# Feature-major queries and keys, and a new order of the work on every engine, in a two-layer attention kernel

## The reference, cut to what matters

```python
h = ln(x);  q, k, v = h@wq+bq, h@wk+bk, h@wv+bv     # 16 heads of 16; q scaled by 0.25
q, k = rope(q), rope(k)                              # rotates halves of each head by the row number
x = x + softmax(q k^T, causal) v @ wo + bo           # self attention
h = ln(x);  q from h;  k, v from y (the context)     # cross attention, rope on q and k, no mask
x = x + softmax(q k^T) v @ wo + bo
x = x + gelu(ln(x) @ fc1 + b1) @ fc2 + b2
w = softmax(x y^T);  out = x + tanh([x, w y] @ W + b)
rope(a) = [a1*cos - a2*sin, a2*cos + a1*sin]         # a1, a2: first and last 8 features of a head
```

## Time and profile before

| | |
|---|---|
| median of three runs | 3020.07 us |
| the profiled execution: time | 3020.76 us |
| the profiled execution: span, first to last instruction | 3019.0 us |
| TensorE matmul busy | 2857.9 us (95%) |
| VectorE busy | 2451.2 us (81%) |
| ScalarE busy | 2043.0 us (68%) |
| GpSimd busy | 1446.1 us (48%) |
| mean granted TensorE clock | 0.987 of 2.4 GHz |
| ScalarE's load of a function table (253 of them) | 1283 ns each |
| VectorE's turn of a bank, `ot_s`, 128x512 from PSUM | 705 ns |
| output store, issue to landing, median | 1.7 us |

### The profile page before, as it was taken

How to read it: one execution, slowest core, us unless ns; L and a number is a source line. 1 busy time by engine, 2 the same in 40 slices (tenths; PEclk the granted TensorE clock), 3 DMA queues, 4 the chain that set the end, 5 groups by cost and what they waited for, 6 DMA issues and landing times.

```text
span 3019.0 us, 92928 instructions
## 1 busy us (share of the span) xinstructions
PE 2857.9 (95%) x38860; PEld 2447.0 (81%) x38860; DVE 2451.2 (81%) x5319; ACT 2043.0 (68%) x4481; POOL 1446.1 (48%) x2180
## 2 busy tenths in 40 slices
PE   3699999999999999999999999999999999999997
PEld 2478888888888888888888888888888888888876
DVE  4598888888888888888888888888888888888873
ACT  0267676776776777767777677777776777776765
POOL 0354454544554555445554554455544544554431
PEclk7799999999999999999999999999999999999999
DMA  3222212222122122221221222212212222122110
GB/s 83 56 51 50 51 46 51 50 50 53 46 51 50 46 52 49 49 53 46 50 51 47 51 49 50 53 46 50 51 46 52 49 49 54 46 50 51 39 30 17
DMA packets 242932, 148.63 MB, mean 49 GB/s; under 512 B 40616, under 2 KB 242216, under 8 KB 242512
## 3 DMA queue, kind: packets, MB, share of 16 engines
q1 hardware_dynamic: 242512, 142.68, 19.9%
HBM read 56.62 MB, written 16.78 MB: 24 GB/s over the span
## 4 chain that ended last, share of the span: by engine, by line
PE 58%; ACT 17%; DVE 15%; DMA 5%; SPq 2%; issue 2%; POOL 1%; POOLq 0%; DVEq 0%; ACTq 0%
ACT pt_c L1042 7%; PE sc L400 7%; PE A L374 6%; PE A L375 6%; PE A L376 6%; DMA qkt_c<-qkst_c 5%; PE A L465 5%; ACT L1042 5%; PE B L597 4%; PE B L375 3%; PE A L369 3%; PE B L374 3%; PE B L376 3%; PE B L603 3%; DVE ct_lo L721 2%; PE A L581 2%
## 5 line engine op out<-in xcount | busy, mean ns | idle before, releaser
L1199 POOL TENSOR_TENSOR rstd<-bmv,eps_t 128x1 f32<-128x1 f32 x384 | 118.7, 309 | 740.8 <-DVE bmv L920 472.2
L1194 POOL TENSOR_TENSOR qkf_s<-tqk,rope_c 128x512 f32<-128x512 f32 x128 | 165.3, 1291 | 546.2 <-DVE tqk L727 546.2
L1042 ACT ACTIVATE pt_s<-sc 128x512 f32<-128x512 f32 x512 | 264.6, 604 | 100.0 <-PE sc L390 100.0
L1201 POOL TENSOR_TENSOR rstd<-rstd,mhalf 128x1 f32<-128x1 f32 x384 | 295.0, 768 | 30.1
L743 DVE TENSOR_REDUCE z_s<-sc 128x8 f32<-128x1024 f32 x256 | 301.7, 1221 | 7.1
L743 DVE TENSOR_REDUCE z_c<-sc 128x8 f32<-128x1024 f32 x256 | 296.6, 1197 | 1.4 <-PE sc L400 1.4
L1042 ACT ACTIVATE pt_c<-sc 128x512 f32<-128x512 f32 x512 | 264.4, 603 | 7.5 <-PE sc L400 6.1
L1204 POOL TENSOR_TENSOR kr_c<-qkt_c,ones_f 128x512 bf16<-128x512 f32 x128 | 137.7, 1076 | 169.8 <-DMA qkt_c<-qkst_c 169.8
L1032 ACT COPY x3t<-B 128x256 f32<-128x256 f32 x128 | 47.7, 373 | 203.6 <-PE B L369 203.6
L1083 ACT ACTIVATE vaug_s<-B,rstd 128x256 f32<-128x256 f32 x128 | 60.9, 476 | 158.8 <-PE B L376 158.7
L1048 ACT ACT_TABLE_LOAD x128 | 164.2, 1283 | 2.3
(11 more groups left out here) (226 smaller groups left out, 10907.9 us busy)
## 6 DMA issues: line engine op xcount, KB each, us to landing
qkt_s<-qkst_s SPq DMA_DIRECT2D x256, 128.0 KB, 2.5
qkt_c<-qkst_c SPq DMA_DIRECT2D x256, 128.0 KB, 2.6
xt_f<-in_x_t SPq DMA_DIRECT2D x128, 128.0 KB, 2.1
rows_in<-in_x SPq DMA_DIRECT2D x128, 128.0 KB, 2.2
rows_in<-in_ctx_t SPq DMA_DIRECT2D x128, 128.0 KB, 2.4
out<-o_out SPq DMA_DIRECT2D x128, 128.0 KB, 1.7
qkt_s<-zt_s SPq DMA_DIRECT2D x512, 2.0 KB
qkt_c<-zt_c SPq DMA_DIRECT2D x512, 2.0 KB
```

What stands on the lines that cost most here:

```text
L1042: act.activation(pt[c][:, r, :, :].rearrange("p g q -> p (g q)"), sc[:, r, :], ACT.Exp).then_inc(signal, 1)
L1194: pool.tensor_tensor(out.rearrange("p (h e) -> p h e", e=HD), t[:, :].rearrange("p (h e) -> p h e", e=HD), rope_c[:, :].unsqueeze(1).broad ...
L1201: pool.tensor_tensor(rstd[k - 1][:, :], rstd[k - 1][:, :], mhalf[:, :], ALU.pow).then_inc(s[f"rstd{k}"], 1)
```

## The change

Queries and keys are made with features on the partitions and rows along the free axis, two tiles at a time. The weights' columns are put in the order "first halves of all heads, then last halves" on the host, so that a rotation is a swap of two blocks of columns. The transposes (`trqk_s_`, `trqk_c_`) and their copies (`qks_`, `qkc_`) go. The bias is now one number per partition and is added by ScalarE as it takes the product out of PSUM.

```diff
-            def trqk_s_(t):
-            def trqk_c_(t):
...
+            def pair_projection(bank, w, c0, a_hi, a_lo):
+                for h in range(2):
+                    c = c0 + h
+                    for k in range(KC):
+                        mm = split3(bank[:, h * E:(h + 1) * E], w_hi[w][:, k, c * P:(c + 1) * P], w_lo[w][:, k, c * P:(c + 1) * P],
+                                    a_hi[:, k, :], a_lo[:, k, :], k == 0, k == KC - 1)
+            def sq_(t):
...
+                    pair_projection(B0, "sqk", 2 * ((t - 1) % M), xt_hi, xt_lo).then_inc(s["sq"], 1)
+            def cp_(t):
...
+                    if t % M == 1:
+                        pair_projection(A1, "ckq", 0, ct_hi, ct_lo).then_inc(s["cp"], 1)
+                    else:
+                        pair_projection(A1, "ckq", 2, x2t_hi, x2t_lo).then_inc(s["cp"], 1)
...
+            def rotate(c, signal):
+                v = tq[c][:, :].rearrange("p (h j q) -> p h j q", h=2, j=M)
+                dve.tensor_tensor(rw[c][:, :].rearrange("p (h j q) -> p h j q", h=2, j=M), v[:, ::-1, :, :],
+                                  rope_s[:, :, :].unsqueeze(2).broadcast_to([P, 2, M, P]), ALU.mult).then_inc(signal, 1)
...
+            def with_bias(c, t, bank, signal):
+                b = (0 if c == "s" else 4) + 2 * ((t - 1) % M)
+                for h in range(2):
+                    w = act.activation(tq[c][:, h * E:(h + 1) * E], bank[:, h * E:(h + 1) * E], ACT.Identity,
+                                       bias=bias_qk[:, b + h:b + h + 1])
...
+            def cosines(c, signal):
+                pool.tensor_tensor(rp[c][:, :].rearrange("p (a q) -> p a q", q=P), tq[c][:, :].rearrange("p (a q) -> p a q", q=P),
+                                   rope_c[:, :].unsqueeze(1).broadcast_to([P, 2 * M, P]), ALU.mult).then_inc(signal, 1)
...
+            def spread(c, t, first, landed):
+                b = (t - 1) // M % 2 * M
+                for g in range(G):
+                    sp.dma_start(qkt[c][0:P:2, b:b + M, first + g, :],
+                                 rp[c][32 * g:32 * g + 32, :].rearrange("p (h j q) -> p h j q", h=2, j=M)).then_inc(landed, 16)
```

```diff
+            def rbw_(t):
+                    sp.wait_ge(s["rs1"], done(t))
+                    sp.dma_start(rstd_rows[t % 4].unsqueeze(1), rstd1[t % 2][:, :]).then_inc(rbw[t % 2], 16)
+            def rbr_(t):
+                    sp.wait_ge(rbw[t % 2], 16 * (t // 2 + 1))
+                    sp.dma_start(rb[t % 2][:, :], rstd_rows[t % 4].partition_broadcast(P)).then_inc(rbr[t % 2], 16)
+            def xs_(t):
...
+                    dve.tensor_tensor(rows, rows, rb[t % 2][:, :].unsqueeze(1).broadcast_to([P, KC, P]), ALU.mult).then_inc(s["xs"], 1)
+            def x2n_(t):
+                    act.wait_ge(s["rs2"], done(t))
+                    act.activation(x2n[:, :], x1[:, :], ACT.Copy, scale=rstd[1][:, 0:1]).then_inc(s["x2n"], 1)
```

More of the change, by code:

```diff
@@ L329, in _ @@
+            steps(slot, 15)
             for q in st_o:
@@ new lines, in p1c_ @@
+            def p1c_(t):
+                if live(t):
+                    pe.wait_ge(s["qr_c"], done(t))
+                    if t <= 1:
+                        need(pe, s["max_s"], 2 * done(t + 3))
+                    heads(qt["c"], kr["c"], MX, True).then_inc(s["p1c"], 1)
+            def slot(u):
+                f2a_(u - 9)
+                cvt_(u - 4)
+                sq_(u)
+                trx2_(u - 4)
+                p2s_(u - 3)
+                f2b_(u - 9)
+                cp_(u - 3)
+                pv_s_(u - 3)
+                p2c_(u - 6)
+                trfa_(u - 12)
+                trx3_(u - 8)
+                fy0_(u - 12)
+                fy_(u - 12)
+                f1b_(u - 8)
+                p1s_(u - 2)
+                f1a_(u - 8)
+                y_c_(u - 7)
+                pv_c_(u - 6)
+                trf_(u - 11)
+                y_s_(u - 3)
+                fs_(u - 11)
+                vs_(u)
+                p1c_(u - 5)
@@ L1024, in _ @@
-            steps(slot, 11)
+            def slot(u):
+                xt_lo_(u - 1)
+                zt_c_(u - 7)
+                rot_s_(u - 1)
+                x2t_lo_(u - 5)
+                ct_lo_(u - 4)
+                add_s_(u - 1)
+                st3_(u - 9)
+                st1_(u)
+                mv3_(u - 9)
+                frec_(u - 13)
+                cw_(u - 5)
+                mv1_(u)
+                rinv_c_(u - 8)
+                att_c_(u - 8)
+                ot_s_(u - 4)
+                rinv_s_(u - 4)
+                rot_c_(u - 4)
+                norm_c_(u - 8)
+                h3_lo_(u - 9)
+                add_c_(u - 4)
+                x3_(u - 10)
+                att_s_(u - 4)
+                norm_s_(u - 4)
+                max_s_(u - 3)
+                x2_(u - 8)
+                hlb_(u - 9)
+                ot_c_(u - 7)
+                hla_(u - 9)
+                x1_(u - 4)
+                zt_s_(u - 3)
+                fmax_(u - 12)
+                st2_(u - 4)
+                xs_(u)
+                mv2_(u - 4)
+                max_c_(u - 6)
@@ L1188, in _ @@
+                x2n_(u - 3)
+            steps(slot, 15)
         @block.gpsimd
```

1208 lines of the change are left out of this document (553 added, 655 removed).

## The result

The changed kernel takes 3336.45 us (median of 4 runs, 3325.14 to 3343.31) against 3021.48 us for the kernel before beside it: 1.104 times as long, 95% interval 1.1005 to 1.1073. The forecast was 3141 us, range 2910 to 3210. The profiled execution spans 3341.5 us, 322.5 more than before.

The account below looks back on a forecast made before the run. TensorE was taken to bound the old kernel at 22.36 us a slot. 116 slots x (23.1 - 22.36) = 86 us, plus 35 us at the ends, on 3020.8 us gave 3142, set at 3141 us; range 2910 to 3210.

Parts of the forecast that it names:

- the round trip: 1/std written to DRAM and read back before `xs_`: 2.6 us taken for the transfer, costed at nothing in a steady slot.
- the walk: Likeliest case: one new slot followed step by step at rows' durations, giving 3085 to 3200 us, chance 0.46.
- The walk's slot: Steady slot of 23.1 us: 5.5 before VectorE starts, 10.5 its work, 4.3 lost to GpSimd, 2.8 TensorE after.
- the lock: VectorE instructions with both inputs in SBUF and GpSimd's exclude each other; with GpSimd's order 4.3 us lost a slot.
- over 85%: Sign of being right: VectorE's busy share, with TensorE idle some 2.4 us a slot, mostly before `trx3_` and `trf_`.
- TensorE's work: TensorE's busy time in a slot: 21.95 less 0.98 for transposes and 0.3 for `cp_`, 20.7 us in every case.
- The ends: Outside the steady slots: filling 16 to 18 us more, draining 15, setup 3; together 35, between 0 and 60.
- The clock: TensorE's clock taken at full speed; the other end was 7% of 20.7 us, 1.4 us a slot.
- TensorE stays the bound: Rival: less than about 2.1 of the 4.3 us lost falls on the chain; slot 21.2 us, 2921 us, chance 0.24.
- SP's queue becomes the bound: Rival: transfers land in 4.2 us, the maxima sent by `zd_s_` come 0.9 us late; slot 24.0, 3246 us, chance 0.09.
- its longest waits on a DMA: Sign of being wrong: TensorE's longest waits are on a DMA transfer; no size given.

Follow-up runs that it names:

- e13: Changed kernel with ones in place of the read-back 1/std, and only the write kept, as 128 single numbers read by nobody: 3234.25 us.
- e16: Changed kernel with ones in place of the read-back 1/std, and only the write kept, as 4 rows of 128 B read by nobody: 3113.22 us.
- e1: Changed kernel without the write and read-back of 1/std through DRAM, rows multiplied by ones: 3037.81 us, one run.
- e3: Changed kernel without the 1/std write and read-back, and with one of four blocks of GpSimd's cosine product in both attentions: 2934.25 us.
- e2: Changed kernel with one of four blocks of GpSimd's cosine product in both attentions, VectorE's sum taking unrotated rows instead: 3217.09 us.
- e7: Changed kernel with statistics, 1/std and its write one tile ahead, and SP issuing the read-back a slot after the write: 3172.78 us.
- e5: Changed kernel with 1/std turned by a VectorE block transpose and written as 4 rows of 128 B: 3191.52 us.

## Why the prediction was wrong

**The step that failed: the price of the round trip.** The forecast took 1.7 to 4.2 us for each transfer from the store and the spread, said "which lands it at 22, a little before `xs_` wants it", and "costed at nothing in a steady slot". Measured: 7.56 us for the write and 4.9 for the read in an empty slot, a read that SP issues behind its other work, and 1.95 us a slot (24.15 - 22.20) with 78 us of filling: 226 + 78 = 304, against 299 measured. Two things were missed. The nearest rows were transfers of long rows; this one has 128 pieces of 4 bytes, and no row of before has such a thing. It should have been left without an upper bound near 4.2 us. And the step was costed only by when it lands, not by what stands behind it in SP's list: the write alone, read by nobody, costs 196 of the 299 us, at least 121 of them by its pieces (e13, e16).

**The sign was luck.** "Slower" was forecast by the walk, with the trip free. The kernel without the trip, e1, takes 3038 us: 16 us or 0.5% above the kernel before, by a single run. The 3085 to 3200 of the walk does not hold it. What made the changed kernel 10% slower was the term put at nothing.

**The walk's slot.** 23.1 us was forecast for a kernel with a free trip; e1 measures 22.20. Taking GpSimd's long product out gave 0.8 to 0.9 us a slot (e1 to e3, changed kernel to e2), where the forecast had the lock and the order decide 1.9 (23.1 less the 21.2 of the case without them). The instructions grew as said: means of 1.49, 1.17 and 1.79 us. But VectorE is busy 79% and not over 85%, and TensorE's waits are not where the walk had them: e1 has 39.6 us before `trx3_`, over 120 times, released by ScalarE's `xhat` and not by `ot_s`, and 1.1 us for `x`. So the lock lengthens VectorE's instructions by what was forecast, and less than half of what the walk made of it reaches the slot. Which steps of the walk VectorE made up for was not traced.

**TensorE's work.** 20.7 us was said to hold in every case; e3, with no wait, has 21.41. Group by group the removed and added ones cost what was forecast, but others grew by 0.6 us together. `f1b_`, from its start to that of the next group, in e3 and in the kernel before:

```profile
1517.60 0.47 PE L392 MATMUL A<-h_hi,w_f_hi 128*128 128x256 f32 x1
1517.90 0.28 PE L393 MATMUL A<-h_lo,w_f_hi 128*128 128x256 f32 x1
...
1519.09 0.28 PE L394 MATMUL A<-h_hi,w_f_lo 128*128 128x256 f32 x1
1519.31 0.40 PE L421 MATMUL sc<-kr_s,qt_s 31*128 31x128 bf16 x16
```
```profile
1516.46 0.28 PE L374 MATMUL A<-h_hi,w_f_hi 128*128 128x256 f32 x1
1516.59 0.28 PE L375 MATMUL A<-h_lo,w_f_hi 128*128 128x256 f32 x1
...
1517.77 0.28 PE L376 MATMUL A<-h_hi,w_f_lo 128*128 128x256 f32 x1
1517.88 1.02 PE L597 MATMUL B<-w_t,x3t 128*128 128x256 f32 x4
```

1.71 against 1.42 us for the same 12 matmuls. In e3 the first matmul stands 0.30 us ahead of the second, behind `fy_`, and the last 0.22 ahead of `p1s_`; in the kernel before these are 0.13, behind `vs_`, and 0.11, ahead of `fy0_`. So the neighbours of a group, ahead and behind, set what the hand-over costs; the forecast had moved groups at no price. Which neighbour costs what was not tried.

**The ends.** Filling was costed at 16 to 18 us more with a trip of "about 5 us"; it is 118. Of this the trip has 78; the remaining 40 are e1's 309 against 269. Draining was costed at 15 and is nothing.

**The clock** was taken at full. It is 0.98 in the steady stretch; after a wait of 2.20 us that ends at 1518.52 `sq_`'s matmuls stand 0.213 us apart instead of 0.117, and the granted clock from 1515 to 1523 is 0.79. e1 has 1.00 in the steady stretch, so this is part of the trip's 1.95 us, not on top.

**The rivals.** "TensorE stays the bound" (2921) is e3, without the trip and with the short cosine. "SP's queue becomes the bound" (3246, given 0.09) named the right queue, by the maxima's landing. Its real place was the write of 1/std. Of the signs of being wrong, "its longest waits on a DMA" holds at one remove: TensorE's longest wait is for VectorE's `xt_lo`, and VectorE's longest, for `xs_`, from which `xt_hi` and `xt_lo` follow, is for the read-back.

## What to carry to other kernels

Price a small transfer by its pieces, not by its bytes, and by everything that stands behind it in its queue; turn a column into rows on an engine before it is sent. When a transfer is hidden by an early start, look whether the queue is hidden too: e7 hid the latency and kept 135 us. A wait at the head of an in-order list cost next to nothing here, where little behind it was ready; moving it cost 1000 us. A right sign can come from a term that the sum had at nothing, as here.

## What the runs showed of the hardware

- A write from SBUF to DRAM of 128 numbers of 4 bytes lands after 7.56 us, from its issue to the next one of SP that waits for it, in the first slot with one load in between; the same 512 bytes as 4 rows of 128 bytes after 1.58 us (e5). The Trainium skill, page "DMA: Bandwidth & Descriptors", section "Anatomy of one DMA", fits about 2.0 us plus bytes over bandwidth for a DMA issued from GpSimd; by that, as an estimate, 512 bytes would take 2.0 us in any number of pieces. These two went through SP's queue: the 4 pieces come near it, the 128 do not, and the measurement decides.
- The small pieces hold up what the same queue sends next: 3.2 to 3.7 us on the mean to issue the four 64 KB transfers of the cross spread in the nine kernels that write single numbers, 2.7 to 3.0 in the nine others of these runs.
- A VectorE sum with one input in PSUM is not held up by GpSimd's product (`cw`, 399 ns clear of it and 414 under it), one with both in SBUF is (`ct_lo`, 1196 and 864 ns, by how much they overlap).
- The same 12 matmuls take 1.42 or 1.71 us, start to start of the next group, with other neighbours ahead and behind.
